# A closing wait of GpSimd on its last two scatter additions, before the drain that ends its program

## The chip, the core and the metric

The kernel runs on one core of a Trainium2 chip. The metric is the device time of one launch in microseconds; three runs of the kernel before gave 551.60, 551.62 and 552.42 us, with a median of 551.62 us.

## What is computed

A gated cross-attention block followed by a gated mixture-of-experts block, in fp32, for x of shape 4 x 512 x 256:

```
x = x + tanh(g_xattn) * (attention(layernorm(x), ctx; 16 heads) @ W_proj + b_proj)
xf = layernorm(x)                                     (2048 tokens x 256)
comb = softmax over the top 2 of 8 router logits, 0 elsewhere
out  = sum over experts e of comb[:, e] * (silu(xf @ wg[e].T) * (xf @ wu[e].T)) @ w_down[e].T
x = x + tanh(g_ffn) * (shared expert(xf) + out)
```

Each token goes to two of the eight experts. The kernel sorts the token-expert pairs into blocks of 128 rows that belong to one expert each, computes block after block, and adds each block's rows to the output in memory.

## The kernel before, in words

The program is one block with a program for each engine. The attention part and the shared expert take the first 380 us or so and play no role at the close. What matters here is the loop over the MAX_BLOCKS = 39 expert blocks and what stands behind it.

For block j, GpSimd gathers 128 token rows from the DRAM tensor x_rows into blk_x (gather, line 505; four homes in turn), TensorE transposes them (line 1402) and does the up projection, ScalarE computes the silu (line 704), VectorE the product (line 1024), TensorE the down projection, and VectorE scales the 128 x 256 result into blk_y (line 1031; two homes in turn). GpSimd then issues an indirect DMA with addition that adds the rows of blk_y to the rows of `out` that blk_row names (line 532). Even blocks count their landing on the semaphore by_out[0], odd blocks on by_out[1], 16 counts for one addition. So 39 gathers and 39 additions are issued by GpSimd in all.

Before addition j, GpSimd waits on both by_out semaphores (lines 525 to 530): addition j - 2 must have landed, and on the other semaphore the count that the table adds_before gives, which is 16 more, addition j - 1 included, where the expert changes between the two blocks. Line 531 waits for blk_y.

After its 39th addition GpSimd's program has nothing more. SyncE, which has been idle since it stored the base of the output, waits at the close for all landings: rows_out, out_done (lines 408, 409) and, for both values of s, by_out[s] at 16 * ((MAX_BLOCKS + 1 - s) // 2), which is 320 for s = 0 and 304 for s = 1 (lines 410, 411).

The block's end is shown at line 80 (the `with ExitStack()` of build): there each engine has a DRAIN, which for SyncE, VectorE, ScalarE and TensorE also raises a count that GpSimd collects; GpSimd, once its own DRAIN is over, waits for that count and releases all five engines with two semaphore instructions. The same sequence, at line 1476, opens the program.

Of the kernel before, what the change touches and what calls it, by code (L numbers as in the profile page):

```python
# [41 lines left out]
MAX_BLOCKS = (TOPK * N + E * (P - 1)) // P  # L42
# [28 lines left out]
def build(nc, x, ctxT, g_xattn, g_ffn, w_kv, w_q, w_proj, b_proj, gateT, w_upT, w_downT, out):  # L71
# [8 lines left out]
    with ExitStack() as ctx:  # L80
# [3 lines left out]
        def sem(name):  # L84
            return ctx.enter_context(nc.semaphore(name))
# [215 lines left out]
        by_out = [sem(f"by_out{s}") for s in range(2)]  # L301
# [113 lines left out]
        def _(pool):  # L415
# [85 lines left out]
            def gather(j):  # L501
                home = j % ROW_HOMES
                if j >= ROW_HOMES:
                    pool.wait_ge(bxT_ps, j - ROW_HOMES + 1)
                pool.indirect_dma_start(  # L505
                    out=blk_x[:, home, :], out_offset=None, in_=x_rows[:, :],
                    in_offset=bass.IndirectOffsetOnAxis(ap=blk_token[:, j:j + 1], axis=0)).then_inc(bx_in[home], 16)
# [8 lines left out]
            for j in range(MAX_BLOCKS):  # L516
                if j >= 3 and (j - 3) % EXPERTS_AT_ONCE == 0:
                    n = min(EXPERTS_AT_ONCE, MAX_BLOCKS - j)
                    _, adds = nc.values_load_multi_w_load_instructions(
                        adds_before[0:1, j - 1:j - 1 + n], engines=[pool.engine], min_val=16,  # L520
                        max_val=16 * (BLOCK_PAIRS + 1),
                        skip_runtime_bounds_check_because="a constant of 16 or more, plus 16 where the expert changes")
                if j + ROW_HOMES < MAX_BLOCKS:
                    gather(j + ROW_HOMES)
                if j >= 2:
                    pool.wait_ge(by_out[j % 2], 16 * (j // 2))
                if j in (1, 2):
                    pool.wait_ge(by_out[(j - 1) % 2], 16)
                elif j >= 3:
                    pool.wait_ge(by_out[(j - 1) % 2], adds[(j - 3) % EXPERTS_AT_ONCE])  # L530
                pool.wait_ge(by_sb, j + 1)
                pool.indirect_dma_start(  # L532
                    out=out[:, :], out_offset=bass.IndirectOffsetOnAxis(ap=blk_row[:, j:j + 1], axis=0),
                    in_=blk_y[:, j % 2, :], in_offset=None, compute_op=ALU.add).then_inc(by_out[j % 2], 16)


        @block.scalar
        def _(act):
# [138 lines left out]
            def copy_up(j, s):  # L677
                if j % EXPERTS_AT_ONCE == 0:
                    n = min(EXPERTS_AT_ONCE, MAX_BLOCKS - j)
                    _, loaded = nc.values_load_multi_w_load_instructions(  # L680
                        block_ei[0:1, j:j + n], engines=[act.engine], min_val=0, max_val=E - 1,
                        skip_runtime_bounds_check_because="a count of ends of experts, capped at E - 1 where it is made")
                    for k in range(n):
                        chosen_expert[j + k] = loaded[k]
                if j >= 2:
                    act.wait_ge(bup_ps, 2 * j - 2)
                nc.scalar.copy(up_now[:, s, :, :].rearrange("p c f -> p (c f)"),  # L687
                               w_up[:, bass.ds(chosen_expert.pop(j), 1), :, :].rearrange("p a c f -> p (a c f)")
                               ).then_inc(up_copied, 1)
# [357 lines left out]
        def _(pe):  # L1047
# [340 lines left out]
            def load_experts(j):  # L1388
                n = min(EXPERTS_AT_ONCE, MAX_BLOCKS - j)
                _, loaded = nc.values_load_multi_w_load_instructions(  # L1390
                    block_ei[0:1, j:j + n], engines=[pe.engine], min_val=0, max_val=E - 1,
                    skip_runtime_bounds_check_because="a count of ends of experts, capped at E - 1 where it is made")
                for k in range(n):
                    expert[j + k] = loaded[k]
# [88 lines left out]
```

## Time and profile before

| | us |
|---|---|
| median of three runs | 551.62 |
| the profiled execution, its own time | 551.44 |
| its span, first to last instruction | 549.7 |
| GpSimd busy | 155.3 |
| TensorE busy (matmul) | 518.2 |

The span is 1.74 us shorter than the profiled execution's own time. Engine names in the rows: PE is TensorE, DVE VectorE, ACT ScalarE, POOL GpSimd, SP SyncE; a name with a q behind it (POOLq, SPq) is that engine's own instruction queue, where waits, branches, drains and the issue of transfers run. Those are not counted as busy.

### The profile page before, as it was taken

The page shows a single profiled execution, that of the slowest core. Times are in us where ns is not written, and L with a number is a line of the kernel's source. Part 1 is how long each engine was busy: PE and PEld are TensorE (multiplying, and loading weights), DVE is VectorE, ACT ScalarE, POOL GpSimd, SP SyncE. Part 2 cuts the span into 40 slices and gives each one's busy share as a digit, 9 for nine tenths or more (in the row PEclk, how much of TensorE's full clock was granted, in tenths as well). Part 3 has the DMA queues.
Part 4 walks back from the last instruction along what each step waited for, and adds up shares of the span by engine and source line. Part 5 has one row for each costly group of instructions (what it writes and reads, how often), then busy time and mean ns, then how long its engine had stood idle before and what let it go on. Part 6 is the DMA issues. An engine that isn't in the chain of part 4 may idle for free.

```text
span 549.7 us, 8931 instructions
## 1 busy us (share of the span) xinstructions
PE 518.2 (94%) x2968; PEld 326.6 (59%) x2968; DVE 300.8 (55%) x546; ACT 276.1 (50%) x441; POOL 155.3 (28%) x181
## 2 busy tenths in 40 slices
PE   8967979999999999999989999999999999999992
PEld 7624522333333333334448647669999999999992
DVE  3655676787888787875447487223233333323331
ACT  1734446777777777776553210212444445444430
POOL 4301422332221111111000000201565566566643
PEclk9988989999999999999998699999999999999997
DMA  7879663773556477500004001102334334443432
GB/s 261 283 216 304 208 189 110 183 192 91 163 163 163 122 202 197 120 4 3 19 2 151 3 0 39 45 33 86 59 60 67 67 60 64 64 66 58 68 49 29
DMA packets 44880, 58.59 MB, mean 107 GB/s; under 512 B 6352, under 2 KB 36688, under 8 KB 44336
## 3 DMA queue, kind: packets, MB, share of 16 engines
q1 hardware_dynamic: 29536, 36.12, 23.9%
q0 software_dynamic: 7488, 10.23, 11.9%
q10 hardware_dynamic: 7824, 11.81, 6.4%
q8 instruction: 20, 0.33, 0.3%
q14 instruction: 12, 0.10, 0.1%
HBM read 37.89 MB, written 20.05 MB: 105 GB/s over the span
## 4 chain that ended last, share of the span: by engine, by line
PE 80%; DMA 6%; DVE 5%; ACT 2%; issue 2%; SPq 2%; ACTq 1%; POOLq 0%; POOL 0%
PE ps L1049 64%; PE ps L1135 11%; DMA out<-unit_region 2%; DMA x_sb<-in_x 2%; PE ps L1143 2%; PE ps L1402 1%; DVE neg_max L764 1%; DVE rows L733 1%; ACT ctx_region L626 1%; DMA v_rows<-dn_region 1%; SPq L343 1%; DVE stats L721 1%; DVE dn_region L758 1%; SPq L327 1%; DMA qk_parts<-up_region 1%
## 5 line engine op out<-in xcount | busy, mean ns | idle before, releaser
L764 DVE TENSOR_REDUCE neg_max<-ps 128x2 f32<-128x1024 f32 x128 | 150.9, 1219 | 44.0 <-PE ps L1049 43.9
L626 ACT ACTIVATE ctx_region<-ps 128x512 f32<-128x512 f32 x256 | 140.1, 596 | 59.8 <-PE ps L1049 59.3
L1049 PE MATMUL ps<-unit_region 96*128 96x512 bf16 (+1 forms) x512 | 136.1, 387 | 13.4 <-DVE neg_max L764 6.0
L1049 PE MATMUL ps<-unit_region,ctx_region 128*128 128x128 f32 (+1 forms) x968 | 113.8, 274 | 0.0
L1049 PEld LDWEIGHTS ps<-unit_region 96*128 96x128 bf16 (+1 forms) x512 | 48.1, 99 | 108.8 <-ACT ctx_region L626 59.0
L1049 PEld LDWEIGHTS ps<-unit_region,ctx_region 128*128 128x128 f32 (+1 forms) x968 | 110.5, 189 | 0.6 <-issue 0.6
L1049 PE MATMUL ps<-dn_region,unit_region 128*128 (+1 forms) x330 | 78.2, 379 | 0.0
L532 POOL DMA_INDIRECT out<-unit_region x39 | 61.9, 1586 | 55.6 <-DMA out<-unit_region 52.4
L505 POOL DMA_INDIRECT unit_region<-x_rows,unit_region x39 | 38.7, 991 | 128.8 <-DVE unit_region L1003 86.9
L687 ACT COPY ctx_region<-up_region 128x1536 f32 x39 | 57.3, 1472 | 34.7 <-PE ps L1049 32.7
L1135 PE MATMUL ps<-ctx_region,unit_region 128*32 128x512 f32 x512 | 69.1, 611 | 1.6 <-ACT ctx_region L626 0.7
L1024 DVE TENSOR_TENSOR unit_region<-unit_region,ps 128x384 f32<-128x384 f32 x39 | 21.6, 553 | 83.1 <-ACT unit_region L704 62.0
L1049 PEld LDWEIGHTS ps<-dn_region,unit_region 128*128 128x128 f32 x330 | 59.7, 190 | 7.8 <-issue 1.4
L704 ACT ACTIVATE unit_region<-ps 128x384 f32<-128x384 f32 x39 | 19.2, 491 | 61.7 <-PE ps L1049 60.4
L470 POOL CAST nm_parts<-nmT 16x128 bf16<-16x128 f32 x16 | 4.5, 281 | 143.4 <-ACT nmT L614 143.4
L1049 PE MATMUL ps<-xnT,up_region 128*128 128x512 f32 x96 | 44.6, 621 | 0.0
L1031 DVE TENSOR_SCALAR unit_region<-ps,unit_region 128x256 f32<-128x256 f32 x39 | 18.9, 484 | 27.0 <-PE ps L1049 27.0
L1049 PEld LDWEIGHTS ps<-xnT,up_region 128*128 128x128 f32 x96 | 18.9, 201 | 21.9 <-issue 21.6
L673 ACT ACTIVATE unit_region<-ps 128x512 f32<-128x512 f32 x12 | 7.2, 597 | 44.3 <-PE ps L1049 44.3
L1135 PEld LDWEIGHTS ps<-ctx_region,unit_region 128*32 128x32 f32 x512 | 10.4, 108 | 21.7 <-issue 20.6
L1143 PEld LDWEIGHTS ps<-ident,o_sb 128*128 128x128 f32 x64 | 8.9, 141 | 15.6 <-issue 14.3
L1049 PE MATMUL ps<-wp_sb,xnT 128*128 128x256 f32 x64 | 16.4, 385 | 1.3 <-DVE xnT L856 1.3
(141 smaller groups left out, 422.3 us busy)
## 6 DMA issues: line engine op xcount, KB each, us to landing
up_region<-in_w_upT ACTq DMA_DIRECT2D x9, 768.0 KB, 4.3
qk_parts<-up_region SPq DMA_DIRECT2D x32, 192.0 KB, 3.2
unit_region<-qk_parts SPq DMA_DIRECT2D x32, 192.0 KB, 4.4
v_rows<-dn_region SPq DMA_DIRECT2D x4, 1024.0 KB, 5.6
unit_region<-qk_parts SPq DMA_DIRECT2D x32, 128.0 KB, 4.3
unit_region<-v_rows SPq DMA_DIRECT2D x16, 256.0 KB, 5.0
dn_region<-in_w_downT ACTq DMA_DIRECT2D x9, 384.0 KB, 5.2
ctx_region<-in_ctxT SPq DMA_DIRECT2D x4, 512.0 KB, 10.7
```

The lines of the kernel that those rows point to most:

```text
L505: pool.indirect_dma_start(out=blk_x[:, home, :], out_offset=None, in_=x_rows[:, :], in_offset=bass.IndirectOffsetOnAxis(ap=blk_token[:, j: ...
L532: pool.indirect_dma_start(out=out[:, :], out_offset=bass.IndirectOffsetOnAxis(ap=blk_row[:, j:j + 1], axis=0), in_=blk_y[:, j % 2, :], in_ ...
L626: nc.scalar.activation(probs[:, k % 8, :], bank(4 + k % 2), ACT.Exp).then_inc(exp_done, 1)
L673: nc.scalar.activation(sh_gate[:, f, :], bank(f), ACT.Silu).then_inc(sh_silu, 1)
L687: nc.scalar.copy(up_now[:, s, :, :].rearrange("p c f -> p (c f)"), w_up[:, bass.ds(chosen_expert.pop(j), 1), :, :].rearrange("p a c f -> p ...
L704: nc.scalar.activation(blk_gate[:, :], bank(2 * (j % 2))[:, 0:HALF], ACT.Silu).then_inc(bsilu, 1)
L764: nc.vector.tensor_reduce(neg_max[:, s, 2 * p:2 * p + 2], bank(2 * (p % 2), 2), AX.X, ALU.max, negate=True).then_inc(max_done, 1)
L1024: nc.vector.tensor_tensor(blk_h[:, s, :], blk_gate[:, :], bank(2 * s + 1)[:, 0:HALF], ALU.mult).then_inc(bhid, 1)
L1031: nc.vector.tensor_scalar(blk_y[:, s, :], bank(6 + s)[:, 0:D], blk_weight[:, j:j + 1], None, ALU.mult).then_inc(by_sb, 1)
L1049: return nc.tensor.matmul(o_, w, m, start=start, stop=stop)
L1135: last = nc.tensor.matmul(bank(6)[h * VW:(h + 1) * VW, :], v_unit[:, s, kt, h * VW:(h + 1) * VW], probs[:, (kt * HG + h) % 8, :], start=kt ...
L1143: last = nc.tensor.transpose(bank(7)[:, qt * P:(qt + 1) * P], o_sb[:, s, qt * P:(qt + 1) * P], ident[:, :])
```

## The change

At the end of GpSimd's program, after the loop over the blocks, two waits are added: the same two that SyncE has at lines 410 and 411. Nothing else is changed.

```diff
                 pool.indirect_dma_start(
                     out=out[:, :], out_offset=bass.IndirectOffsetOnAxis(ap=blk_row[:, j:j + 1], axis=0),
                     in_=blk_y[:, j % 2, :], in_offset=None, compute_op=ALU.add).then_inc(by_out[j % 2], 16)
+            for s in range(2):
+                pool.wait_ge(by_out[s], 16 * ((MAX_BLOCKS + 1 - s) // 2))
```

## Rows read from the trace of the kernel before

**Rows 1.** The chain that ended last, from 530 us on: start us, us, what.

```profile
527.26 3.88 DMA out<-unit_region
531.13 0.32 issue
531.46 3.72 DMA out<-unit_region
535.18 0.44 issue
535.62 3.83 DMA out<-unit_region
539.44 0.14 issue
539.58 0.58 POOL out L532
540.17 0.49 issue
540.66 2.34 POOLq L80
```

**Rows 2.** The instructions of line 80 at the block's end: duration ns min/median/max, first and last start.

```profile
L80 POOLq EVENT_SEMAPHORE  x2: 17/17/17, 549.5 to 549.6; - x2
...
L80 PEldq DRAIN  x1: 1582/1582/1582, 538.0 to 538.0; - x1
L80 DVEq DRAIN  x1: 524/524/524, 539.6 to 539.6; - x1
L80 POOLq DRAIN  x1: 8777/8777/8777, 540.7 to 540.7; - x1
L80 SPq COMPARE_BRANCH  x1: 38/38/38, 545.2 to 545.2; - x1
L80 SPq DRAIN  x1: 7/7/7, 545.4 to 545.4; - x1
L80 SPq EVENT_SEMAPHORE  x1: 17/17/17, 549.6 to 549.6; - x1
```

**Rows 3.** The timeline from 538 us on: start us, us, engine, line, operation, out<-in [idle before].

```profile
539.58 1.55 POOL L532 DMA_INDIRECT out<-unit_region  x1 [2.42 <-DMA out<-unit_region]
539.61 0.48 DVE L1031 TENSOR_SCALAR unit_region<-ps,unit_region 128x256 f32<-128x256 f32 x1 [0.81 <-PE ps L1049]
541.44 1.55 POOL L532 DMA_INDIRECT out<-unit_region  x1 [0.30 <-issue]
```

**Rows 4.** Line 532's instructions in the window from 541 us on.

```profile
DMA to landing us min/median/max: 3.6/3.6/3.6
```

**Rows 5.** SyncE's closing waits at line 411, from 500 us on.

```profile
L411 SPq EVENT_SEMAPHORE  x2: 17/22/28, 545.1 to 545.1; - x2
```

**Rows 6.** Stretches of the close: us, busy (x) per engine, PEclk, DMA share, GB/s.

```profile
543.00:545.10 2.10, 0.00 (x0) 0.00 (x0) 0.00 (x0) 0.00 (x0) 0.00 (x0) 0.50 0.53 62
545.10:549.70 4.60, 0.00 (x0) 0.00 (x0) 0.00 (x0) 0.00 (x0) 0.00 (x0) 0.50 0.00 0
```

**Rows 7.** GpSimd's last wait for blk_y, line 531, from 538 us on.

```profile
L531 POOLq EVENT_SEMAPHORE  x2: 42/42/43, 538.8 to 540.1; - x2
```

**Rows 8.** GpSimd's drain and others of line 1476, at the program's start.

```profile
L1476 DVEq DRAIN  x1: 10/10/10, 0.1 to 0.1; - x1
...
L1476 SPq DRAIN  x1: 7/7/7, 0.2 to 0.2; - x1
...
L1476 POOLq DRAIN  x1: 194/194/194, 0.4 to 0.4; - x1
```

**Rows 9.** All transfers that GpSimd issues: out<-in, queue, operation xcount, median us to landing.

```profile
unit_region<-x_rows,unit_region POOLq DMA_INDIRECT x39
out<-unit_region POOLq DMA_INDIRECT x39, 3.9
```

## The prediction

> **What bounds the close now.** The change adds two waits behind GpSimd's last instruction, so only the last 10 us can differ. I read the chain of waits first [rows 1]: the additions to the output follow each other in steps of about 4.2 us, each released by a landing, and the last piece is GpSimd's queue at line 80, the block's end. The instructions of line 80 say what that is [rows 2]: a DRAIN of 8.777 us that starts at 540.66 [rows 1] and so ends at 549.44. Behind it stand only GpSimd's two semaphore instructions of 17 ns at 549.5 and 549.6, and the release of the others at 549.6. SyncE's own waits for the landings are over at 545.1 [rows 5], its DRAIN is at 545.4 and takes 7 ns [rows 2], and then it stands still for 4.2 us. So the end is set by GpSimd's drain and not by the landing that SyncE waits for.
>
> The drain has three pieces. Up to 542.99 GpSimd is still working on its last addition, which starts at 541.44 and takes 1.55 [rows 3]. A drain does wait for its own engine: VectorE's starts at 539.6, takes 0.524, and its last operation ends at 539.61 + 0.48 = 540.09 [rows 2, 3]. That is 2.33 us of the 8.78. From 542.99 to the landing at 541.44 + 3.6 = 545.04 [rows 3, 4] the drain may be waiting for the transfer or may be doing work of its own: 2.05 us. From 545.04 to 549.44, 4.40 us, nothing is in flight: the DMA share is 0.53 in the stretch before and 0.00 in this one, and no engine is busy [rows 6]. Of the 6.45 us after the engine came free, 4.40 are therefore certainly not spent waiting for a transfer to land. What they are spent on no row shows.
>
> **The change part by part.** It removes nothing. It adds two waits on semaphores that reach their counts when the last two additions land. Behind them on GpSimd's queue stand only the DRAIN and the two closing semaphore instructions; for these all five engines wait. No transfer, no engine work and no gather is behind them, and the last addition has been issued, so nothing earlier moves.
>
> Step 1, when the drain can start. The last landing is at 545.04. SyncE, with the same waits, has its wait at 545.1 and its DRAIN at 545.4 [rows 2, 5], 0.3 to 0.4 after the landing, with a branch between. GpSimd's queue took longer between its last wait for blk_y at 540.1 and the DRAIN at 540.66, 0.5 us, with the issue of an addition between [rows 1, 7]. So the drain starts 0.3 to 0.5 us after the landing, at 545.35 to 545.55. I take 545.4, by SyncE's row, since its instructions are the same ones. The two waits themselves are 17 to 28 ns each, inside these 0.36 us.
>
> Step 2, how long the drain then takes. No row shows a drain that begins after the landing, so I bound it from both sides. The lower end is the drain of a queue with nothing behind it: GpSimd's at the start, 0.19 us, or the 0.01 us of the others there [rows 8]. The upper end is the whole 8.78 us [rows 2]. Between them stand 4.40 (what followed the landing) and 6.45 (what followed the engine's last work). I take 6.45, for this reason. The start's drain, when GpSimd had issued no transfer, is the only cheap one; at the end it has issued 39 gathers and 39 additions [rows 9]. If the drain goes through its own 78 transfers one after the other and looks at each, that is 6.45 / 78 = 83 ns each, an estimate from these rows. Work of this kind starts when the engine is free, runs beside the landing, and reaches the last two transfers when they have long landed. It explains why the end comes nowhere near a landing. With the change this same work no longer lies beside the landing but behind it.
>
> Sum: drain from 545.4 to 551.85 instead of to 549.44, which is +2.41 us. The release behind it (0.2 us) stays. The profiled execution's 551.44 becomes 553.85; the median of the runs is 0.18 above that execution, so I forecast **554.0 us**. The bounds of step 1 make it 553.9 to 554.1, and with 0.5 for the spread of runs (551.60 to 552.42 before) 553.6 to 554.6 is this case's own range.
>
> **A rule against it.** The rows of the start give 7 to 10 ns for SyncE's and VectorE's drain and 194 ns for GpSimd's [rows 8]; those of the end give 7 ns for SyncE's and 8777 ns for GpSimd's [rows 2]. The Trainium skill ("VectorE: DVE Perf Modes", section "The DRAIN you can't avoid") says that the drains of preamble and postamble are about 12 ns constant, on all five engines. By it a drain costs only what it waits for, and the time would be that of the second rival below. The trace agrees for SyncE and disagrees for GpSimd, whose drain lasted 4.40 us with nothing in flight.
>
> **The rivals.**
>
> First, no difference. The drain's work is in series behind the last landing (a clean-up that needs the transfers complete): before it was 545.04 + 4.40, with the change it is 545.4 + 4.40 = 549.8, so +0.36 us, 552.0. For it: the last transfers were not landed when the engine came free, and a drain that waits for its engine may well wait for its transfers first. Against it: nothing but the arithmetic; it needs a fixed 4.40 us after completion, where SyncE's drain has 7 ns behind its own transfers [rows 2].
>
> Second, faster. The 4.40 us are the price of a drain that meets unfinished transfers: it looks, finds them open, and looks again much later, or goes through a slow path. If all has landed before it starts, it finds all closed at the first look and is as short as at the start: 545.4 + 0.19 instead of 549.44 is -3.85 us, 547.8. If it is as short as VectorE's 0.52, 548.1. For it: the only drain of GpSimd with nothing open is 45 times shorter [rows 2, 8]. Against it: that one also came before any transfer at all, and a re-look that comes 4.40 us after a wait of 2.05 is a long interval. A weaker form, with two looks of 3.2 us (half of 6.45) where one would do, gives 545.4 + 3.2 = 548.6, -0.8 us, 550.8; it is in the range and counts as no difference. It becomes a gain as soon as the drain after the wait is shorter than 549.44 - 545.4 = 4.0 us; that is the point from which this rival decides.
>
> Third, slower by more. The drain's work starts with its queue instruction at 540.66, beside the engine's last addition, and all 8.78 us are its own: 545.4 + 8.78 = 554.2, +4.7 us, 556.3. Against it: VectorE's drain ends right behind its engine's last work [rows 2, 3], so waiting for the engine is the likelier first piece.
>
> That the change does nothing, since SyncE waits for the same landings anyway, would need GpSimd's drain to be the same wait under another name; it ends 4.40 us after that wait is over, so I give that no place of its own.
>
> **How the numbers follow.** Forecast 0.52, no difference 0.20 (the weaker form in it), the second rival 0.22, the third 0.06. Two parts in a thousand, 1.1 us, is about what a measurement of this kernel can tell from no change. Faster: 0.22. Same: 0.20. Slower: 0.52 + 0.06 = 0.58. The range has to reach to the fast rival, since without it more than 2 in 10 would be left out: 547.7 to 554.6. It leaves out the third rival and the tails. Cases of both signs hold most of the chance, so the likeliest one's own range is the one above, 553.6 to 554.6.
>
> **What the profile after would show.** Step 1: GpSimd's DRAIN at line 80 starts at about 545.4 instead of 540.66, and so after the waits of the new line. Step 2: its duration. About 6.4 us says that its work is fixed and was partly hidden beside the landing; about 4.4 that it stood in series behind the landing; 0.2 to 0.5 that it was a price of open transfers; 8.8 the third rival. The last addition should start at 541.4 and land 3.6 us later as before; if the steps of 4.2 us between additions moved, the whole argument from the close would be wrong.

## The result, and the profile after

| us | before | changed |
|---|---|---|
| median of five runs each | 552.39 (551.60 to 552.75) | 554.90 (553.37 to 556.24) |
| ratio, 95% interval | 1 | 1.0050 (1.0028 to 1.0071) |
| the profiled execution, its own time | 551.44 | 553.37 |
| its span | 549.7 | 551.6 |
| GpSimd's closing drain: start, duration | 540.66, 8.78 | 544.9, 6.43 |

The change makes the kernel 2.5 us slower, where the forecast had 2.4 us. The measured 554.9 us nevertheless lies above the forecast of 554.0 and above its range, which ends at 554.6; the reason is the level of the runs, taken up below.

The chain of waits of the changed kernel, from 530 us on (start us, us, what); it answers to [rows 1]:

```profile
535.36 3.71 DMA out<-unit_region
539.07 0.26 issue
539.33 0.58 POOL out L532
539.91 1.27 issue
541.18 1.55 POOL out L532
```

The chain ends here with GpSimd's last addition; the drain behind it is found at its line. The instructions of line 80 at the block's end, of the new line 536 and of SyncE's waits (duration ns min/median/max, first and last start), the landing of the last addition at line 532, and the stretch behind that landing (us, busy time of each engine, TensorE's clock, DMA share, GB/s); they answer to [rows 2, 4, 5, 6]:

```profile
L80 POOLq EVENT_SEMAPHORE  x2: 17/17/17, 551.4 to 551.5; - x2
L80 DVEq DRAIN  x1: 524/524/524, 539.4 to 539.4; - x1
L80 POOLq COMPARE_BRANCH  x1: 41/41/41, 544.8 to 544.8; - x1
L80 POOLq DRAIN  x1: 6430/6430/6430, 544.9 to 544.9; - x1
L80 SPq DRAIN  x1: 7/7/7, 545.1 to 545.1; - x1
...
L536 POOLq EVENT_SEMAPHORE  x1: 17/17/17, 543.1 to 543.1; - x1
...
L411 SPq EVENT_SEMAPHORE  x2: 17/22/28, 544.8 to 544.8; - x2
...
DMA to landing us min/median/max: 3.6/3.6/3.6
...
545.10:551.60 6.50, 0.00 (x0) 0.00 (x0) 0.00 (x0) 0.00 (x0) 0.00 (x0) 0.50 0.00 0
```

The reader should see three things. One of the added waits is over at 543.1, which is when the last addition but one (an odd block) lands; the other, carried by the branch of line 80, is over at 544.8, in the same 0.1 us as SyncE's. The drain starts at 544.9, 0.2 us behind the landing at 541.18 + 3.6 = 544.78. And it takes 6.430 us, where the kernel before had 6.45 us from the end of its engine's last work (542.99) to the drain's end (549.44). The whole of it moved behind the landing. With nothing in flight (DMA share 0.00 in the last row) and every landing already waited for, it was no shorter.

### The profile page after: what moved, and what is told of

Same layout as the page of the kernel before. It is cut to its first block, busy times and chain, and to the rows that moved or that the text cites. A ratio compares the mean times of both kernels' runs of the same rounds, so it can differ in the third digit from the quotient of the medians.

```text
span 551.6 us, 8933 instructions
## 1 busy us (share of the span) xinstructions
PE 518.1 (94%) x2968; PEld 326.4 (59%) x2968; DVE 300.7 (55%) x546; ACT 276.0 (50%) x441; POOL 155.0 (28%) x181
## 4 chain that ended last, share of the span: by engine, by line
PE 64%; DMA 20%; DVE 5%; issue 3%; ACT 2%; SPq 2%; ACTq 1%; POOL 0%; POOLq 0%
PE ps L1051 50%; DMA out<-unit_region 16%; PE ps L1137 11%; DMA x_sb<-in_x 2%; PE ps L1145 2%; DVE neg_max L766 1%; DMA v_rows<-dn_region 1%; DVE rows L735 1%; ACT ctx_region L628 1%; SPq L343 1%; DVE stats L723 1%; PE ps L1404 1%; SPq L327 1%; DMA qk_parts<-up_region 1%; DMA unit_region<-qk_parts 0%
```

## The experiments

**The change again, and its half.** The first run repeats the change. The second keeps one of its two waits:

```diff
-            for s in range(2):
-                pool.wait_ge(by_out[s], 16 * ((MAX_BLOCKS + 1 - s) // 2))
+            pool.wait_ge(by_out[1], 16 * (MAX_BLOCKS // 2))
```

> The changed kernel once more, beside the kernel before on the same chip. Theory A (GpSimd's closing drain is work of its own, about 6.45 us from when the engine is free, and not a wait for landings): the drain takes 6.4 us and starts 0.2 us behind the last landing; the kernel is 2.0 to 2.7 us slower than the kernel before on this chip, ratio 1.0036 to 1.0049. Theory B (the 554.9 holds something besides the close, since the five runs lay between 553.4 and 556.2): the difference comes out clearly away from 2.4 us, or the trace shows a difference before 540 us too.

Measured: 554.52 us (12 runs) beside 552.19 for the kernel before (29 runs, 548.52 to 554.09) on that chip: ratio 1.0047 (1.0024 to 1.0069), 2.3 us. The drain takes 6430 ns again. Theory B falls: the difference is that of theory A.

> Only the wait for the odd blocks' semaphore, so for the last addition but one, which lands some 1.8 us before the last. Theory A: the drain can start 0.2 us behind that landing, at about 543.3, just after the engine comes free at 543.0; it takes 6.4 us whatever is still in flight, and ends at about 549.8: 0.1 to 0.5 us slower than the kernel before, no difference that can be measured. Rival C (the change costs time because the closing drain is slow in a queue that has just waited on a semaphore): 2 us slower or more, as in the changed kernel.

Measured: 553.23 us (10 runs), ratio 1.0023 (1.0003 to 1.0042), 1.0 us. The timeline of its last two additions, the drain at line 80 and SyncE's waits:

```profile
541.48 1.55 POOL L532 DMA_INDIRECT out<-unit_region  x1 [2.41 <-DMA out<-unit_region]
...
543.33 1.55 POOL L532 DMA_INDIRECT out<-unit_region  x1 [0.30 <-issue]
...
L80 POOLq DRAIN  x1: 6430/6430/6430, 545.5 to 545.5; - x1
...
L411 SPq EVENT_SEMAPHORE  x2: 17/22/28, 547.0 to 547.1; - x2
```

The engine comes free at 543.33 + 1.55 = 544.88 and the drain starts at 545.5, 0.6 us later, where 0.1 to 0.5 was expected; that is the price of this half of the wait in the trace, and the timed 1.0 us agrees with it within its interval. More telling is the duration. The last addition lands at 547.0, 1.5 us into this drain, and the drain still takes 6430 ns, to the nanosecond as long as with nothing open. Rival C is out: waiting on a semaphore first does not slow the drain. It also shows that at least the first 1.5 us of the drain's work can lie ahead of the last landing.

**The drain left out.** The block is opened without GpSimd's closing drain; SyncE's waits still cover every landing:

```diff
-        block = ctx.enter_context(nc.Block())
+        block = ctx.enter_context(nc.Block(no_gpsimd_drain=True))
```

> The kernel before, its block opened without the closing drain of GpSimd; SyncE still waits for every landing. Theory A: the end is then set by SyncE's waits, 0.4 us behind the last landing, plus 0.2 for the release: the span ends at 545.7 instead of 549.7, 3.8 to 4.1 us faster, 548.4. Rival D (what takes 6.4 us is not the drain instruction but something behind it, which the next instruction of the queue would then pay for): no gain.

Measured: 548.07 us (6 runs), ratio 0.9932 (0.9906 to 0.9957), 4.1 us faster. Line 80 and SyncE's waits of this run:

```profile
L80 SPq EVENT_SEMAPHORE  x2: 17/17/17, 546.5 to 546.7; - x2
L80 POOLq EVENT_SEMAPHORE  x2: 17/17/17, 546.5 to 546.6; - x2
...
L411 SPq EVENT_SEMAPHORE  x2: 17/22/28, 546.1 to 546.2; - x2
```

No POOLq DRAIN is left, and the release at 546.7 is 0.6 us behind SyncE's first wait. Rival D is out, and this is the version that beats both kernels. The same with the two waits of the change kept:

> The changed kernel, its two added waits kept, with the closing drain of GpSimd left out. If the added waits cost only because the drain stands behind them: 3.8 to 4.3 us faster than the kernel before, as without the drain and without the waits. If the waits have a price of their own: less of a gain by that price.

Measured: 548.38 us (5 runs), ratio 0.9929 (0.9907 to 0.9951). Without the drain behind them the added waits cost nothing that these runs can tell (3.9 us gained here, 4.1 without the waits); they cost what they put off.

**What the 6.43 us consist of.** The forecast estimated 83 ns for each transfer that GpSimd has issued. The first test added transfers, 39 small ones of zeros to a scratch tensor, while GpSimd idles ahead of the gathers:

```diff
             pool.wait_ge(resid_base, NT)
+            for i in range(39):
+                pool.dma_start(extra[i, :, :], empty[:, 0, 4 * i:4 * i + 4]).then_inc(extra_out, 16)
+            pool.wait_ge(extra_out, 16 * 39)
```

> The kernel before with 39 more small transfers issued by GpSimd (zeros, 2 KB each, to a scratch tensor in DRAM) while it idles between the residual adds and the gathers, all landed before the gathers. Theory A1 (the drain goes through every transfer that GpSimd has issued, 83 ns each): 117 instead of 78 transfers make the drain's own part 9.7 instead of 6.45 us, the kernel 3.2 us slower. Theory A2 (a fixed piece of work, whatever the number): the drain ends as before, 6.45 us behind the engine's last work, and the time is the same within 0.5 us.

Measured: 552.0 us (10 runs), ratio 1.0005 (0.9981 to 1.0029); the drain takes 8785 ns, 8 ns more than before. That spoke for a fixed piece of work. The next three runs measured drains elsewhere; each of these, and of all runs below, was timed once, so that durations in the trace count and small differences in time do not. Four drains in the idle stretch:

```diff
             pool.wait_ge(resid_base, NT)
+            pool.drain()
+            done = 0
+            for n in (39, 0, 1):
+                for i in range(done, done + n):
+                    pool.dma_start(extra[i, :, :], empty[:, 0, 4 * i:4 * i + 4]).then_inc(extra_out, 16)
+                done += n
+                pool.wait_ge(extra_out, 16 * done)
+                pool.drain()
```

> Four drains of GpSimd's queue, all in its idle time between the residual adds and the gathers: the first when it has issued no transfer yet, the second after 39 small transfers (all landed), the third at once behind the second, the fourth after one more small transfer. Theory E (a drain costs 6.4 us as soon as there has been a transfer since the last drain, whatever their number): 0.2, 6.4, 0.2, 6.4 us, and 6.4 at the close. Theory F (6.4 us once GpSimd has ever issued a transfer): 0.2, 6.4, 6.4, 6.4, 6.4. Theory G (every drain but the one at the very start costs 6.4 us, transfers or not): 6.4 for all. The time is that of the kernel before in all three, since GpSimd idles there for longer than the sum.

The four drains by line, first that of line 501, then the three of line 508:

```profile
L501 POOLq DRAIN  x1: 41/41/41, 258.2 to 258.2; - x1
...
L508 POOLq DRAIN  x3: 34/129/3248, 281.1 to 287.1; - x3
```

None of the three theories had this. After no transfer 41 ns, after 39 transfers 3248, directly behind that 34, after one more 129: the fixed price is about 0.03 us, and (3248 - 34) / 39 is 82.4 ns for each transfer. So theory A1 was right about the price, and A2, E, F and G fall. The closing drain of this run takes 8775 ns, as before, with 78 transfers since the last drain; the time is 549.56 us.

> The kernel before with a second drain directly ahead of the closing one. Theory E: the first takes 8.8 us, the second 0.2, and the time is the same within 0.5 us. Theories F and G: the second takes another 6.4 us and the kernel is 6.5 us slower, 558.5.

Measured: the added drain takes 8777 ns, the closing one behind it 47 ns, and the single time is 551.25 us. A drain clears what it has gone through. The edit is one `pool.drain()` behind the loop.

> The kernel before with one more drain of GpSimd's queue in the block loop, ahead of the wait for block 20's rows, when 25 gathers and 20 additions have been issued. Theories E, F and G: this drain takes 6.4 us plus what GpSimd still has running, the closing one 8.8 us as before, and the kernel is 3 to 6.5 us slower, since GpSimd has some 2.6 us of slack in a block. If the cost had gone with the transfers issued since the last drain (45 here, 33 at the close), both would be shorter than 6.4: 3.7 and 2.7.

Measured: 550.89 us, within the scatter of the kernel before (550.89 to 553.46 on that chip). The edit is `if j == 20: pool.drain()` ahead of line 531. The gather that GpSimd's engine is still working on when the first drain begins, and its landing; the last addition; the drains and SyncE's waits by line:

```profile
466.97 0.99 POOL L505 DMA_INDIRECT unit_region<-x_rows,unit_region  x1 [0.30 <-issue]
...
DMA to landing us min/median/max: 3.2/3.2/3.2
...
543.64 1.55 POOL L534 DMA_INDIRECT out<-unit_region  x1 [0.30 <-issue]
...
L532 POOLq DRAIN  x1: 6671/6671/6671, 465.4 to 465.4; - x1
...
L80 POOLq DRAIN  x1: 6032/6032/6032, 542.9 to 542.9; - x1
...
L411 SPq EVENT_SEMAPHORE  x2: 17/22/28, 547.5 to 547.6; - x2
```

From the end of the engine's last work (466.97 + 0.99 = 467.96 and 543.64 + 1.55 = 545.19) these are 4.1 and 3.7 us; 45 and 33 transfers at 82.4 ns would be 3.7 and 2.7. The cost does go with the count, since the closing drain is shorter than before, but something else adds 0.4 and 1.0. To see whether that is the open transfers, the changed kernel, whose closing drain already stands behind waits for every addition, was given a drain at block 20 behind such waits:

```diff
+                if j == 20:
+                    pool.wait_ge(by_out[(j - 1) % 2], 16 * (j // 2))
+                    for h in range(ROW_HOMES):
+                        pool.wait_ge(bx_in[h], 16 * ((j + ROW_HOMES - h) // ROW_HOMES + 1))
+                    pool.drain()
                 pool.wait_ge(by_sb, j + 1)
```

> The changed kernel with one more drain in the block loop at block 20, there too behind waits for all landings, so that neither drain meets an open transfer. 25 gathers and 20 additions stand before the first, 14 and 19 between the first and the closing one. Theory H (82.5 ns for each transfer issued since the last drain, whatever its kind): 3.7 us and 2.7 us. Rival I (a price by something else, as the 4.1 and 3.7 us suggest that the two drains of the mid-drain run took from when the engine was free): 4.1 and 3.7 again.

```profile
L535 POOLq DRAIN  x1: 3735/3735/3735, 470.5 to 470.5; - x1
...
L80 POOLq DRAIN  x1: 2737/2737/2737, 551.3 to 551.3; - x1
```

Theory H holds: 45 x 82.4 + 34 is 3742 and 33 x 82.4 + 34 is 2753. The time was 555.99 us (552.6 for the kernel before on that chip). The excess of the run before belongs to transfers still open when the drain met them.

The numbers on record fit a drain whose work comes in two halves, with the wait for the last landing between them. No run was made to test this. Half the price is 41.2 ns. The closing drain of the run before would be through its first half at 545.19 + 33 x 0.0412 = 546.55, would wait for the landing that SyncE sees at 547.5, and would need 1.36 us more, to 548.9; it ends at 542.9 + 6.0 = 548.9. The one at block 20 would be through its first half at 467.96 + 45 x 0.0412 = 469.8; the gather issued at 466.97 lands 3.2 us later, at 470.2, and 1.85 us more is 472.0; it ends at 465.4 + 6.7 = 472.1. In the kernel before the first half, 78 x 0.0412 = 3.2 us from 542.99, outlasts the landing at 545.04, and with one wait it outlasts the one at 547.0, so neither has an excess.

**Does a drain wait for landings at all?** With the added drain at block 37 only two additions are left for the closing one:

> The kernel before with one more drain ahead of the wait for block 37's rows, when all gathers and 37 additions have been issued; two additions stand between it and the closing drain. Theory H: the first takes about 6.3 us of its own. The closing drain has 0.17 us of work, far less than the landing takes, so it shows whether a drain waits for landings at all: if yes, it ends 0.1 to 0.2 us behind the last landing, if no, 0.2 us behind the engine's last work and 2 us before SyncE's waits. The kernel is 2 to 4 us faster at the close and loses up to 6 us at the first drain.

The drain at line 532, the last additions, the closing drain and SyncE's waits:

```profile
L532 POOLq DRAIN  x1: 7975/7975/7975, 535.6 to 535.6; - x1
...
535.78 1.55 POOL L534 DMA_INDIRECT out<-unit_region  x1 [2.59 <-DMA out<-unit_region]
544.33 1.55 POOL L534 DMA_INDIRECT out<-unit_region  x1 [6.99 <-issue]
546.18 1.55 POOL L534 DMA_INDIRECT out<-unit_region  x1 [0.31 <-issue]
...
L80 POOLq DRAIN  x1: 5208/5208/5208, 544.7 to 544.7; - x1
...
L411 SPq EVENT_SEMAPHORE  x2: 17/22/28, 549.8 to 549.8; - x2
```

The first drain ends at 535.6 + 8.0 = 543.6, 6.3 us after the engine's 535.78 + 1.55, and 76 transfers at 82.4 ns are 6.3. The closing one, with two transfers of 0.08 us each, takes 5.2 us and ends at 544.7 + 5.2 = 549.9, 0.1 us behind SyncE's waits at 549.8. So a drain does wait for landings: the changed kernel waits on semaphores for what its drain would have waited for anyway, and in the kernel before that wait was hidden whole in the 6.45 us. The time, 552.01 us, is close to that of the kernel before (552.6 on that chip): what the short closing drain saved, the one at block 37 took.

**Why 39 more transfers cost nothing.** Two runs put the 39 transfers and the drains differently. In the first they stand early as before, with a drain ahead of the first gather some 65 us later; in the second they are issued directly ahead of the gathers.

> The 39 small extra transfers again, and a drain not directly behind them (it took 3.25 us there) but some 65 us later, ahead of the first gather. Theory J (what a queue has issued is cleared by itself while it idles, which is why 39 extra transfers before that idle stretch cost the closing drain nothing): 0.04 us. Rival K (there is a ceiling near 78 transfers on what one drain goes through): 3.25 us again.

Measured: 3254 ns, and 553.04 us. The 65 us of idle time cleared nothing; theory J falls.

> The 39 small extra transfers issued directly ahead of the first gather, with no idle stretch behind them. Theory J: all 117 count at the close, the closing drain's own part is 9.6 us instead of 6.45. Rival K: 6.45 again. The extra transfers stand in front of the gathers here and put off the loop by up to 21 us, so only the drain's duration is to be read, not the time.

Measured: the closing drain takes 8788 ns, so 6.45 us from the engine's last work, with 117 issued. The time, 551.16 us, shows none of the delay that was thought possible. Rival K seemed to be it. Two last runs, with 84 transfers of both kinds and then 120 small ones ahead of a drain:

> The changed kernel with the 39 small extra transfers early and the drain at block 20 behind waits for all landings, when 39 + 45 = 84 transfers have been issued. If every transfer since the last drain counts, its duration is 84 times 82.5 ns, 6.9 us. Rival K (a ceiling near 78): 6.4 us. Rival L (issuing gathers or additions clears the small early ones): 3.7 us. The closing drain has 33 transfers and 2.7 us in all three.

Measured: 6928 ns, 84 x 82.4 + 34 being 6956, and 2741 ns for the closing drain. There is no ceiling at 78 and nothing is cleared on the way to 84. The time was 560.98 us, beside 551.85 for the kernel before; this drain behind waits in the middle of the loop cost some 9 us, in one run.

> The changed kernel with 120 small transfers early and a drain directly behind them. If all count: 120 times 82.5 ns, 9.9 us. Rival K (a ceiling near 78 transfers): 6.4 us. The closing drain takes 6.4 us in both, since only the loop's 78 stand before it.

The time was 552.42 us and the closing drain took 6425 ns. The drain at line 504, and the small transfers, all 120 at line 502, in the timeline:

```profile
L504 POOLq DRAIN  x1: 641/641/641, 328.8 to 328.8; - x1
...
258.88 60.75 POOL L502 DMA_DIRECT2D extra<-empty  x113 [0.33 <-POOL nm_parts L478]
323.86 3.72 POOL L502 DMA_DIRECT2D extra<-empty  x7 [4.24 <-issue]
```

641 ns are (641 - 34) / 82.4 = 7.4 transfers, and 7 is what stands behind the pause of 4.24 us. So 113 transfers went out, issuing stopped for 4.24 us, and the drain had the last 7: the 113 had been cleared by then. With 39 small ones ahead of the 78, transfer 114 is the addition of block 35 (39 + 39 gathers + 35 additions are 113). In the run with the early 39 that addition is the one at 532.03, 4.71 us after the one before it, while the kernel before has 4.20 there [rows 1]. Last, the same two additions in the run where a drain ahead of the first gather had cleared the 39:

```profile
527.32 1.59 POOL L537 DMA_INDIRECT out<-unit_region  x1 [1.32 <-DMA out<-unit_region]
532.03 1.56 POOL L537 DMA_INDIRECT out<-unit_region  x1 [3.12 <-DMA out<-unit_region]
...
528.90 1.59 POOL L538 DMA_INDIRECT out<-unit_region  x1 [1.32 <-DMA out<-unit_region]
533.10 1.56 POOL L538 DMA_INDIRECT out<-unit_region  x1 [2.61 <-DMA out<-unit_region]
```

Cleared beforehand, the step is 4.20 us again, as it is in the run with four drains; with the late 39 it is 4.70. So the 0.5 us come with the 114th transfer since the last drain. The closing drain's 6.45 us are those of 78 transfers, so 39 of the 117 had been cleared. That it happened in this pause is inferred. Why 39 there and 113 in the other run was not tried. Nor does the drain's price hold for such a pause: 4.24 us for 113 are 38 ns each, and 0.5 us for 39 are 13.

## Why the prediction missed, and what of it held

**What bounds the close** held. Leaving out the drain gave 4.1 us, within 0.1 of the 4.04 that lie between SyncE's DRAIN at 545.4 and the end of GpSimd's at 549.44 [rows 2].

**Step 1** was a little off: 0.36 us was taken from the landing to the drain's start, by SyncE's rows, and it is 0.2. GpSimd's second wait is carried by its branch, so it has one instruction less in between than SyncE.

**Step 2** held: 6.45 taken, 6.43 measured, and the reason given for choosing it over 4.40 and 0.19, work on each of the 78 transfers, was the right one, with 83 ns estimated for each and 82.4 measured. The wait for the landing was hidden whole only because there was enough of this work; in the mid-loop run it was not. The estimate left out that a pause clears transfers once 113 are issued, which is not reached here.

**The sum** was +2.41 us. In the traces it is 2.2, from 8.0 to 10.2 us between the start of the last addition and the drain's end, and the timed differences are 2.5 and 2.3.

**The failed step** is the one from the sum to the median and its range. It took 551.62, the median of three runs, as the level and allowed 0.5 us for the spread, because those three lay within 0.8 us. Five runs put that level at 552.39, and the 29 runs of the experiments lie between 548.52 and 554.09. The measured 554.90 is 552.39 + 2.5: of the 0.9 us between forecast and result 0.8 are the level and 0.1 the difference. The forecast of the difference was right; the term for the level was 0.8 us too low and its allowance too small, and the range, wide towards the fast rival, had only 0.6 us on the side of the forecast. The runs differ ahead of the close: the last addition starts at 541.18 in one profile of the changed kernel and at 542.83 in another, and the drain is 6430 ns in both.

**The rivals.** No difference: the work is not all in series behind the landing. It starts when the engine is free, and a drain that began 1.5 us ahead of the last landing took the same 6430 ns; by the fit above half of it does wait for the landing, but the other half, 3.2 us, covers the 2.05 us until then. Faster: open transfers are not what makes the drain long; with all landed it is as long. The Trainium skill ("VectorE: DVE Perf Modes", "The DRAIN you can't avoid") gives about 12 ns for the drains of preamble and postamble. The drain here goes with an option of the kernel's own block, so the page need not mean it; it took 34 to 47 ns with no transfer behind it and 6430 with 78. Slower by more: the drain waits for its own engine first, as taken.

## What to carry to other kernels

A drain of GpSimd's queue is work that grows with the number of transfers it has issued since the last drain. Before putting a wait ahead of it, ask what of that work now runs beside the thing waited for: here 2 us did, and the wait took them out of hiding. Where another engine already waits for every landing, leaving such a drain out gave 4.1 us here; whether a program launched afterwards needs it was not tried. A drain earlier in the loop does shorten the closing one, but at blocks 20 and 37 no gain in time was seen.

## What the runs showed of the hardware that was not expected

- A drain of GpSimd's queue took 0.034 us plus 0.082 us for each transfer issued since the last drain: 34 to 47 ns for none, 129 for 1, 2737 and 2741 for 33, 3248 and 3254 for 39, 3735 for 45, 6425 and 6430 for 78, 6928 for 84. Indirect transfers of 128 rows and plain ones of 2 KB cost the same.
- It also waits for landings. With two transfers since the last drain it ended 0.1 us behind the last landing, with 33 it ended 1.4 us behind; both fit half of its work standing behind the landing, which was not tested further.
- 65 us of idle time did not clear issued transfers. In a row of small ones the 114th came after a pause of 4.24 us, behind which only the last 7 counted; among the indirect ones it came 0.5 us late.
